# GPS graph layer on one core: the wait for a chunk's gathered rows moved from ScalarE to VectorE

## The chip, the cores and the metric

The kernel runs on one core of one Trainium2 chip (trn2). The metric is the device time of one execution in microseconds (us), the median of three runs. One more execution was recorded by the hardware profiler; all rows in this text are from that one. Engines are named as in the profile: PE (TensorE matrix unit; PEld is its weight load), DVE (VectorE), ACT (ScalarE), POOL (GpSimd), SP (SyncE). A "q" behind the name (DVEq, ACTq, POOLq) is the sequencer of that engine, which handles register, branch and semaphore instructions alone.

## The reference, cut to what matters

The layer adds three things to 6250 node rows of 256 features: a graph attention over 200,000 edges (sorted by destination), a global attention ("mix") and a mixture-of-experts block. The part around the change is the graph attention, together with the mix features that share its loop:

```python
xw = (x @ W).reshape(N, H, C)                 # N = 6250, H = 8, C = 32
e = leaky_relu(a_src[src] + a_dst[dst], 0.2)  # one logit per edge and head
ex = exp(e - m[dst])
alpha = ex / (segment_sum(ex, dst)[dst] + EPS)
out = segment_sum(xw[src] * alpha[:, :, None], dst)   # per destination node
# and per node row of the mix: features of q (products of q with itself), times a fixed matrix
```

The kernel uses, in place of the segment maximum m, a bound per destination (leaky_relu of a_dst plus the largest a_src), and divides once at the end.

## The kernel before, in words

The execution has stages, each a block of its own: weights and statistics, node rows (projection, `node_rows` written to HBM), a short list stage, then the **edge loop** (lines 786 to 1108), then the expert gating, the experts and the last normalisation. The change is in the edge loop.

The sorted edges are cut into 392 chunks of 512 edges (4 tiles of 128). Destinations are cut into 49 blocks of 128 nodes. A chunk that straddles two blocks is worked on once for each, so there are 440 steps (`STEPS`) for 392 chunks. For step s three small tables made by the list stage tell what to take: `blk_row[s]` (the block), `slot_row[s]` (in which of the 4 slots of `rows_g` the chunk lies) and `need_row[s]` (how many chunks must have landed: the chunk's number plus one). An engine reads an entry into a register with `value_load`; the profile shows such a read as TENSOR_LOAD with a few register instructions around it, on the line of the `value_load`.

What each engine does in the loop, in its program order:

- POOL (lines 864 to 890) gathers the source rows. For each chunk it waits until the step that used the slot last has made its messages (`msg_ready`, from DVE), waits for the indices (`idx_in`), issues 4 indirect DMAs (L876, one for each tile of 128 rows of 264 floats), then waits for the landing of the chunk before (`gathered`) and adds one to `chunks_in` (L881).
- SP (L897) loads the index lists, four chunks ahead.
- DVE (`body`, lines 995 to 1015) does for step s: reads `blk_row` (L964) and `slot_row` (L999); `select(s+1)`, four comparisons that make the 0/1 matrix `sel_bf` of the next step (L959); waits for `dst_spread` (the destinations' logits of step s, from PE) and makes the logits `lg` from the gathered rows (L1005, L1007, L1009; `logit_ready`); adds the sums of step s-2 to `acc` (L969); makes one mix feature (`qfeat`, L355); waits for the exponentials (`weight_ready`, from ACT) and makes the messages `msg` (L1015, `msg_ready`).
- ACT (`body`, lines 930 to 944) does for step s: `take_turned(s+1)`, which reads `need_row[s+1]` (L918), waits for `chunks_in` (L919), waits for PE's transposed selection and copies it to `sel_t` (L922); the exponential of the logits of step s (L935); `widen(s+1)`, a copy of `sel_bf` as float32 (L915); the copy of the transposed mix feature (L928). ACT itself reads no gathered row.
- PE (`body`, lines 1075 to 1103) does: `turn(s+1)`, the transposes of `sel_bf` (L1030, `sel_turned`); `aggregate(s-1)`, the sums of messages (L1051, `msg_summed`); transposes of the mix feature (L1058, `feat_turned`); `spread(s+1)`, 12 small products that bring the destinations' logits to the edges (L1042, `dst_spread`); the products of the mix features (L1071).

The last 40 steps have no mix features. The order of the work is set by these programs, written out by hand; nothing is scheduled by a planner. The logits of step s can read the rows safely today because `dst_spread` of step s comes from PE's `spread(s)`, which waits for ACT's `sel_t` copy of step s, which stands behind the chunk wait.

Of the kernel before, what the change touches and what calls it, by code (L numbers as in the profile page):

```python
# [31 lines left out]
CHUNKS = 392  # L32
# [29 lines left out]
def wait(eng, sem, value):  # L62

    if isinstance(value, int) and value <= 0:
        return
    eng.wait_ge(sem, value)
# [48 lines left out]
def gps_layer(nc, x, src, dst, gnn_W, att_src, att_dst, gnn_bias, Wqkv, bqkv, Wproj, bproj, temperature,  # L115
# [3 lines left out]
    def sb(name, shape, dt=F32, ctx=None):  # L119
        return (ctx or top).enter_context(nc.sbuf_tensor(name, shape, dt))  # L120
# [4 lines left out]
    def sem(name, ctx=None):  # L125
        return (ctx or top).enter_context(nc.semaphore(name))

    with top:
# [492 lines left out]
        need_row = sb("need_row", [1, SP_], I32, ctx=early)  # L621
# [165 lines left out]
        with ExitStack() as c:  # L787
# [32 lines left out]
            chunks_in = sem("chunks_in", c)  # L820
# [29 lines left out]
            def units(k):  # L850

                return (H - 1, H) if k == OCT - 1 else (k,)

            def pe_st(j):
                return p_st[:, (j % 2) * TC * P:(j % 2 + 1) * TC * P]

            def p_e(j):
                return p_eb[:, (j % 2) * TC * 2 * H:(j % 2 + 1) * TC * 2 * H]
# [46 lines left out]
            @block.scalar  # L905
            def _(act):
                def query(t):

                    wait(act, q_doubled, t)
                    act.dma_start(qs[:], qn_dram[bass.ts(t, P), :]).then_inc(q_in, 16)  # L910

                def widen(s, j):
                    act.wait_ge(sel_ready, s + 1)
                    wait(act, msg_summed, s - 1)
                    act.copy(sel[j % 2][:], sel_bf[j % 2][:].rearrange("p u d -> p (u d)")).then_inc(sel_wide, 1)  # L915

                def take_turned(s, j):
                    need = act.value_load(need_row[0:1, bass.ds(s, 1)], min_val=1, max_val=CHUNKS)  # L918
                    act.wait_ge(chunks_in, need)  # L919
                    act.wait_ge(sel_turned, s + 1)  # L920
                    wait(act, dst_spread, s - 1)
                    act.copy(sel_t[j % 2][:], pe_st(j)).then_inc(sel_t_ready, 1)  # L922

                def take(n, u):

                    act.wait_ge(feat_turned, n + 1)
                    wait(act, feat_t_used, n - 2)
                    act.copy(feat_t[u % 3][:], p_ft[u % 2][:]).then_inc(feat_t_ready, 1)  # L928

                def body(s, k, tile, last):  # L930
                    j = k % R
                    take_turned(s + 1, j + 1)
                    wait(act, msg_summed, s - 1)
                    act.wait_ge(logit_ready, s + 1)
                    act.activation(msg[j % 2][:, :, D:ROW], lg[j % 2][:], ACT.Exp).then_inc(weight_ready, 1)  # L935
                    widen(s + 1, j + 1)
                    if last is not None and k == 3:
                        act.wait_ge(yt_in_psum, last + 1)
                        act.copy(yt[:], p_o[:, 0:D]).then_inc(yt_ready, 1)
                    if tile is not None:  # L940
                        for u in units(k):
                            take(tile * UNITS + u, u)
                        if k == 1:
                            query(tile + 1)

                query(0)
                widen(0, 0)
                take_turned(0, 0)
                rounds(act, body)
                act.wait_ge(q_in, (T + 1) * 16)  # L950

            @block.vector
            def _(dve):
                def select(s, j):

                    wait(dve, sel_wide, s - 1)
                    wait(dve, sel_turned, s - 1)
                    for u in range(TC):
                        a = dve.tensor_scalar(sel_bf[j % 2][:, u, :], iota_bf[:], dst_t[:, bass.ds(s, 1), u:u + 1].rearrange("p s u -> p (s u)"),  # L959
                                              None, ALU.is_equal)  # L960
                    a.then_inc(sel_ready, 1)

                def block_of(s):
                    return dve.value_load(blk_row[0:1, bass.ds(s, 1)], min_val=0, max_val=T - 1)  # L964

                def accumulate(s, j, b):
                    a = acc[:, bass.ds(b, 1), :].rearrange("p a f -> p (a f)")
                    dve.wait_ge(msg_summed, s + 1)
                    dve.tensor_tensor(a, a, p_m[j % 2][:, 0:ROW], ALU.add).then_inc(acc_added, 1)  # L969

                def query(k, tile, last):
                    if last is not None and k == 1:
                        dve.wait_ge(feat_t_used, last * UNITS + UNITS)
                        y3 = p_y[:, 0:H * V1].rearrange("p (h e) -> p h e", h=H)
                        dve.reciprocal(ry[:], y3[:, :, 0])
                        dve.drain()
                        dve.tensor_tensor(yn[:].rearrange("p (h e) -> p h e", h=H), y3[:, :, 1:V1],
                                          ry[:].unsqueeze(2).broadcast_to([P, H, C]), ALU.mult).then_inc(y_taken, 1)
                    if last is not None and k == 5:
                        r = resid[:, bass.ds(last, 1), :].rearrange("p a f -> p (a f)")  # L980
                        dve.wait_ge(mix_ready, last + 1)
                        dve.tensor_tensor(r, r, p_o[:, 0:D], ALU.add).then_inc(mix_added, 1)
                        dve.drain()
                        dve.tensor_tensor(r, r, b_proj[:], ALU.add)
                    if tile is not None:
                        if k == 0:
                            dve.wait_ge(q_in, tile * 16 + 16)
                            dve.tensor_copy(qq[:, :, 0:C], qs[:].rearrange("p (h e) -> p h e", h=H))
                            dve.tensor_copy(qq[:, :, C:WRAP], qs[:].rearrange("p (h e) -> p h e", h=H)[:, :, 0:WRAP - C]).then_inc(q_doubled, 1)
                            dve.drain()  # L990
                        for u in units(k):
                            wait(dve, feat_turned, tile * UNITS + (u - 2))
                            products(dve, feat[u % 3][:], qq, u).then_inc(feat_ready, 1)

                def body(s, k, tile, last):
                    j = k % R
                    if not (isinstance(s, int) and s < 2):
                        b = block_of(s - 2)
                    slot = dve.value_load(slot_row[0:1, bass.ds(s, 1)], min_val=0, max_val=R - 1)  # L999
                    select(s + 1, j + 1)  # L1000
                    dve.wait_ge(dst_spread, s + 1)
                    g3 = rows_g[:, bass.ds(slot, 1), :, :].rearrange("p a u f -> p (a u) f")
                    pe3 = p_e(j).rearrange("p (u a) -> p u a", u=TC)
                    l = lg[j % 2]
                    dve.tensor_tensor(l[:], g3[:, :, D:ROW], pe3[:, :, 0:H], ALU.add)  # L1005
                    dve.drain()
                    dve.scalar_tensor_tensor(out=l[:], in0=l[:], scalar=SLOPE, in1=l[:], op0=ALU.mult, op1=ALU.max)  # L1007
                    dve.drain()
                    dve.tensor_tensor(l[:], l[:], pe3[:, :, H:2 * H], ALU.subtract).then_inc(logit_ready, 1)  # L1009
                    if not (isinstance(s, int) and s < 2):  # L1010
                        accumulate(s - 2, j - 2, b)
                    query(k, tile, last)
                    dve.wait_ge(weight_ready, s + 1)
                    m4 = msg[j % 2][:, :, 0:D].rearrange("p u (h e) -> p u h e", h=H)
                    dve.tensor_tensor(m4, g3[:, :, 0:D].rearrange("p u (h e) -> p u h e", h=H), msg[j % 2][:, :, D:ROW].unsqueeze(3).broadcast_to([P, TC, H, C]), ALU.mult).then_inc(msg_ready, 1)  # L1015

                select(0, 0)
                rounds(dve, body)
                for s in (STEPS - 2, STEPS - 1):
                    dve.drain()  # L1020
                    accumulate(s, s % R, block_of(s))
                dve.drain()
# [676 lines left out]
```

## Time and profile before

| what | us |
|---|---|
| median of 3 runs | 4702.44 |
| lowest and highest of them | 4685.48 and 4721.66 |
| profiled execution: span from the first to the last instruction | 4647.3 |
| of it, the edge loop's stretch (590 to 3740) | 3150 |

Of the profiled execution only the span is known; what lies around it (start and end of the execution) is the rest of its own time. The span is 55.1 us below the median of the runs. In the profile, the span of an engine's instruction counts as busy; what it waits for is inferred from semaphore events. "remote" is a wait that ended with a semaphore event for which no instruction was found that had just ended; "issue" is idle time with no wait found behind it.

### The profile page before, as it was taken

What the parts mean: (1) busy time and instruction counts of PE and PEld (TensorE: products, weight loads), DVE (VectorE), ACT (ScalarE), POOL (GpSimd) and SP (SyncE); (2) the same over time, 40 slices, a digit from 0 to 9 for tenths busy, and PEclk for the clock granted to TensorE, in tenths of its full rate; (3) what the DMA queues carried; (4) which work ended last, traced back from release to release, by engine and by line L of the source; (5) the groups of instructions that cost most, each with busy time, mean ns of one, the idle gap of its engine ahead of it and who ended that gap; (6) DMA issues with size and microseconds to landing.
All of it is one profiled execution on the core that took longest, in us unless ns stands there. A gap on an engine that the chain in (4) does not pass through costs nothing. (4 is left out here: it accounts for less than half of the span.)

```text
span 4647.3 us, 81992 instructions
## 1 busy us (share of the span) xinstructions
PE 3345.3 (72%) x20995; PEld 2712.4 (58%) x20996; DVE 2450.8 (53%) x6646; ACT 1123.2 (24%) x2618; POOL 2191.8 (47%) x2161
## 2 busy tenths in 40 slices
PE   5888567777777777777778777787776542599950
PEld 2444256666666666666666666666664442488840
DVE  6999745455555555555545545555454484211127
ACT  2333122222222222222222222222222210122210
POOL 3777454544545555444445444454445546200035
PEclk9999767777878787777877777777877755799975
DMA  3000122222222222222222222222222212577743
GB/s 107 28 30 29 24 74 70 69 70 68 71 68 72 71 73 68 69 69 70 71 65 70 70 68 68 68 69 69 70 68 76 70 30 87 190 230 233 235 144 117
DMA packets 276264, 390.98 MB, mean 84 GB/s; under 512 B 113615, under 2 KB 188654, under 8 KB 276184
## 3 DMA queue, kind: packets, MB, share of 16 engines
q0 software_dynamic: 91088, 256.16, 19.7%
q1 hardware_dynamic: 177784, 127.59, 9.4%
q10 hardware_dynamic: 7344, 6.69, 0.5%
q8 instruction: 18, 0.29, 0.0%
q14 instruction: 30, 0.25, 0.0%
HBM read 336.26 MB, written 55.58 MB: 84 GB/s over the span
## 5 line engine op out<-in xcount | busy, mean ns | idle before, releaser
L876 POOL DMA_INDIRECT rows_g<-node_rows,idx x1568 | 1562.5, 996 | 1609.1 <-DVE msg L1015 1131.3
L1051 PE MATMUL p_m<-msg,sel 128*128 128x264 f32 x3520 | 1196.5, 496 | 18.4 <-issue 17.1
L1051 PEld LDWEIGHTS p_m<-msg,sel 128*128 128x128 f32 x3520 | 830.7, 248 | 191.6 <-issue 32.6
L1015 DVE TENSOR_TENSOR msg<-rows_g,msg 128x1024 f32<-128x1024 f32 x440 | 539.4, 1226 | 368.7 <-ACT msg L935 347.3
L1058 PE MATMUL p_ft<-ident,qfeat 128*128 128x128 f32 x1800 | 351.2, 329 | 436.1 <-DVE qfeat L355 386.5
L1005 DVE TENSOR_TENSOR lg<-rows_g,p_e 128x32 f32<-128x32 f32 x440 | 81.1, 184 | 956.1 <-remote 811.8
L1058 PEld LDWEIGHTS p_ft<-ident,qfeat 128*128 128x128 f32 x1800 | 265.9, 175 | 529.3 <-DVE qfeat L355 438.2
L922 ACT COPY sel_t<-p_st 128x512 bf16<-128x512 bf16 x441 | 258.0, 585 | 1254.7 <-remote 814.1
L1071 PE MATMUL p_y<-mix_w,qfeat_t 128*128 128x33 f32 x3200 | 547.4, 324 | 9.3 <-issue 9.3
L1071 PEld LDWEIGHTS p_y<-mix_w,qfeat_t 128*128 128x128 f32 x3200 | 513.4, 244 | 35.5 <-ACT qfeat_t L928 19.8
L915 ACT CAST sel<-sel_bf 128x512 f32<-128x512 bf16 x441 | 270.6, 614 | 688.5 <-PE p_m L1051 408.0
L959 DVE TENSOR_SCALAR sel_bf<-iota_bf,dst_t 128x128 bf16<-128x128 bf16 x1764 | 330.4, 267 | 132.3 <-issue 124.0
L928 ACT COPY qfeat_t<-p_ft 128x512 f32<-128x512 f32 x450 | 263.2, 585 | 408.7 <-PE p_ft L1058 243.7
L1042 PE MATMUL p_e<-adm_parts,sel_t 128*128 x5292 | 225.8, 173 | 173.2 <-ACT sel_t L922 114.1
L1042 PEld LDWEIGHTS p_e<-adm_parts,sel_t 128*128 128x128 bf16 x5292 | 219.3, 101 | 217.2 <-issue 199.5
L1030 PE MATMUL p_st<-ident_bf,sel_bf 128*128 128x128 bf16 x1764 | 210.9, 253 | 103.7 <-DVE sel_bf L959 82.3
L355 DVE TENSOR_TENSOR qfeat<-qq 128x512 f32<-128x512 f32 x400 | 275.0, 688 | 8.9 <-issue 8.6
L1581 POOL DMA_DIRECT2D slot_y<-ysb x64 | 34.6, 541 | 462.9 <-DVE ysb L1571 462.9
L355 DVE TENSOR_TENSOR kfeat<-kk 128x512 f32<-128x512 f32 x250 | 252.9, 1043 | 0.1
L1524 PE MATMUL e_ph<-xst,wa 128*128 128x256 f32 x1024 | 234.5, 382 | 3.5 <-DMA bb<-in_L_ffn_b_dram 2.6
L1533 PE MATMUL e_py<-wb,ht 128*128 128x256 f32 x1024 | 231.4, 379 | 0.0
L1030 PEld LDWEIGHTS p_st<-ident_bf,sel_bf 128*128 128x128 bf16 x1764 | 156.1, 128 | 117.2 <-DVE sel_bf L959 93.1
(294 smaller groups left out, 3816.5 us busy)
## 6 DMA issues: line engine op xcount, KB each, us to landing
wa<-in_L_ffn_w_dram SPq DMA_DIRECT2D x64, 512.0 KB, 3.9
wb<-in_L_ffn_w_dram SPq DMA_DIRECT2D x64, 512.0 KB, 5.2
rows_g<-node_rows,idx POOLq DMA_INDIRECT x1568
xs<-slot_x SPq DMA_DIRECT2D x64, 256.0 KB, 3.2
slot_y<-ysb POOLq DMA_DIRECT2D x64, 256.0 KB, 4.4
bb<-in_L_ffn_b_dram SPq DMA_DIRECT2D x64, 128.0 KB, 5.2
node_rows<-row SPq DMA_DIRECT2D x50, 132.0 KB, 1.8
qs<-qn_dram ACTq DMA_DIRECT2D x51, 128.0 KB
```

Of the source, the lines that this page charges most:

```text
L355: return eng.tensor_tensor(feat.rearrange("p (d i) -> p d i", i=C), bass.AP(base.tensor, base.offset, [whole, [0, DIAGS - 1], [1, C]]), ba ...
L876: pool.indirect_dma_start(rows_g[:, j, u, :], None, node_rows, bass.IndirectOffsetOnAxis(ap=idx[j][:, u:u + 1], axis=0)).then_inc(gathered ...
L915: act.copy(sel[j % 2][:], sel_bf[j % 2][:].rearrange("p u d -> p (u d)")).then_inc(sel_wide, 1)
L922: act.copy(sel_t[j % 2][:], pe_st(j)).then_inc(sel_t_ready, 1)
L928: act.copy(feat_t[u % 3][:], p_ft[u % 2][:]).then_inc(feat_t_ready, 1)
L959: a = dve.tensor_scalar(sel_bf[j % 2][:, u, :], iota_bf[:], dst_t[:, bass.ds(s, 1), u:u + 1].rearrange("p s u -> p (s u)"), None, ALU.is_e ...
L1015: dve.tensor_tensor(m4, g3[:, :, 0:D].rearrange("p u (h e) -> p u h e", h=H), msg[j % 2][:, :, D:ROW].unsqueeze(3).broadcast_to([P, TC, H, ...
L1030: mm = pe.transpose(pe_st(j)[:, u * P:(u + 1) * P], sel_bf[j % 2][:, u, :], ident_bf[:])
L1042: mm = pe.matmul(p_e(j)[:, u * 2 * H:(u + 1) * 2 * H], sel_t[j % 2][:, u * P:(u + 1) * P], adm_parts[:, bass.ds(b, 1), part, :].rearrange( ...
L1051: mm = pe.matmul(p_m[j % 2][:, 0:ROW], sel[j % 2][:, u * P:(u + 1) * P], msg[j % 2][:, u, :], start=(u == 0), stop=(u == TC - 1))
L1058: mm = pe.transpose(p_ft[u % 2][:, m * P:(m + 1) * P], feat[u % 3][:, m * P:(m + 1) * P], ident[:])
L1071: mm = pe.matmul(o, feat_t[u % 3][:, m * P:(m + 1) * P], w, start=False, stop=(u == H and m == FCH - 1), skip_group_check=True)
```

## The change

ACT no longer reads `need_row` and no longer waits for `chunks_in` ahead of the `sel_t` copy. DVE reads `need_row[s]` behind `slot_row[s]` (so ahead of `select(s+1)`) and waits for `chunks_in` behind its wait for `dst_spread`, ahead of the first logit instruction of step s.

```diff
                 def take_turned(s, j):
-                    need = act.value_load(need_row[0:1, bass.ds(s, 1)], min_val=1, max_val=CHUNKS)
-                    act.wait_ge(chunks_in, need)
                     act.wait_ge(sel_turned, s + 1)
                     wait(act, dst_spread, s - 1)
                     act.copy(sel_t[j % 2][:], pe_st(j)).then_inc(sel_t_ready, 1)
...
                     slot = dve.value_load(slot_row[0:1, bass.ds(s, 1)], min_val=0, max_val=R - 1)
+                    need = dve.value_load(need_row[0:1, bass.ds(s, 1)], min_val=1, max_val=CHUNKS)
                     select(s + 1, j + 1)
                     dve.wait_ge(dst_spread, s + 1)
+                    dve.wait_ge(chunks_in, need)
                     g3 = rows_g[:, bass.ds(slot, 1), :, :].rearrange("p a u f -> p (a u) f")
```

## Rows read from the trace of the kernel before

**Rows 1.** Busy time by engine in the edge loop's stretch (us, instructions), granted clock.
```profile
590.00:3740.00 3150.00, 2393.03 (x16371) 2011.59 (x16372) 1607.95 (x4755) 840.16 (x1822) 1560.09 (x1566) 0.77 0.27 70
```

**Rows 2.** Who waited for whom in 590:3740: total us, times, longest.
```profile
POOL rows_g L876 <- DVE msg L1015: 1131.3, 226, 11.2
ACT sel_t L922 <- remote: 814.1, 176, 10.5
DVE lg L1005 <- remote: 811.8, 158, 11.5
...
ACT sel_t L922 <- PE p_st L1030: 395.4, 223, 3.4
...
DVE msg L1015 <- ACT msg L935: 347.3, 209, 7.4
...
DVE lg L1005 <- PE p_e L1042: 130.7, 72, 4.3
DVE sel_bf L959 <- issue: 123.7, 287, 0.9
PE p_e L1042 <- ACT sel_t L922: 114.1, 52, 8.5
...
PE p_st L1030 <- DVE sel_bf L959: 79.3, 70, 2.7
...
ACT sel_t L922 <- issue: 35.3, 37, 4.8
...
ACT sel_t L922 <- POOLq L881: 9.7, 2, 7.8
```

**Rows 3.** Timeline 1968:2002: PE's small products, a gather, and two late releases.
```profile
1981.50 0.45 PE L1042 MATMUL p_e<-adm_parts,sel_t 128*128 x12
...
1984.02 0.94 POOL L876 DMA_INDIRECT rows_g<-node_rows,idx  x1 [0.30 <-issue]
1985.99 0.58 ACT L922 COPY sel_t<-p_st 128x512 bf16<-128x512 bf16 x1 [3.63 <-remote]
1986.06 0.19 DVE L1005 TENSOR_TENSOR lg<-rows_g,p_e 128x32 f32<-128x32 f32 x1 [5.51 <-remote]
```

**Rows 4.** Timeline 2000:2017: a pair of steps.
```profile
2003.72 0.46 PE L1042 MATMUL p_e<-adm_parts,sel_t 128*128 x12
...
2005.14 0.94 POOL L876 DMA_INDIRECT rows_g<-node_rows,idx  x1 [4.06 <-DVE msg L1015]
2005.33 0.18 DVE L1005 TENSOR_TENSOR lg<-rows_g,p_e 128x32 f32<-128x32 f32 x1
...
2007.24 1.22 DVE L1015 TENSOR_TENSOR msg<-rows_g,msg 128x1024 f32<-128x1024 f32 x1 [0.22 <-ACT msg L935]
...
2008.86 0.74 DVE L959 TENSOR_SCALAR sel_bf<-iota_bf,dst_t 128x128 bf16<-128x128 bf16 x4 [0.39 <-issue]
...
2014.60 0.95 POOL L876 DMA_INDIRECT rows_g<-node_rows,idx  x1 [0.30 <-issue]
```

**Rows 5.** Lines L999 (read of slot_row) and L918 (read of need_row): ns min/median/max.
```profile
L999 DVEq FUSED_REGOPS  x493: 53/190/210, 585.1 to 3734.5; - x165
L999 DVEq TENSOR_LOAD <-slot_row x440: 297/300/562, 584.5 to 3734.2; - x147
L999 DVEq SEQ_ASSERT  x440: 23/23/35, 585.3 to 3734.7; - x147
L999 DVEq ALU_OP  x371: 40/40/40, 663.6 to 3734.1; - x186
...
L918 ACTq TENSOR_LOAD <-need_row x441: 273/281/481, 585.1 to 3734.5; - x147
```

**Rows 6.** Timeline 593:604: the first step of the loop.
```profile
593.56 0.58 ACT L922 COPY sel_t<-p_st 128x512 bf16<-128x512 bf16 x1 [7.82 <-POOLq L881]
...
597.66 0.19 DVE L1005 TENSOR_TENSOR lg<-rows_g,p_e 128x32 f32<-128x32 f32 x1 [11.52 <-remote]
```

## The prediction, made before the changed kernel ran

> **What bounds the kernel now.** I read four views: busy time by stretch, then who waited for whom, then timelines of single steps, then the two lines that read a table entry into a register. The edge loop takes 3150 us of the span of 4647.3, and no engine fills it: PE 76%, DVE 51%, POOL 50%, ACT 27%, at a mean granted clock of 0.77, so PE goes part of the time at 2.4 GHz and part at 1.2 [rows 1]. With 440 steps that is 7.16 us for one. The loop is bound by hand-overs between engines, and the question is which of them ends last.
>
> Three waits stand out: POOL's gathers wait 1131.3 us for the messages of DVE, ACT's `sel_t` copy waits 814.1 us for "remote", and so does DVE's first logit instruction, 811.8 us [rows 2]. The copy's line is where the chunk wait stands today, so its 814.1 us invite the reading that ACT sits there until gathered rows land. The rows speak against it. DVE's logit instruction has no chunk wait at present, only the one for `dst_spread` of PE, yet it has the same "remote" share. In one case PE's products ended at 1981.95 by the record, the gather that was under way ended at 1984.96, and DVE and ACT both went on at 1985.99 and 1986.06 [rows 3]. The two wait there for different semaphores of PE. With no gather under way it looks otherwise: PE's products ended at 2004.18, the next gather began at 2005.14 and the logit instruction at 2005.33, with no idle time before it [rows 4]. So I read "remote" as semaphores of PE that reach the others only when a run of gathers is over. Where the chunk wait does end last, the releaser has a name, L881, and that is the case 2 times in 441, 9.7 us in all [rows 2], 7.82 of them at the very first step [rows 6].
>
> The steps go in pairs: a release, a message, then two chunks gathered back to back (here from 2005.14 to 2015.55), while PE's semaphores come late [rows 4].
>
> **The change part by part.**
>
> *The wait itself.* On ACT it costs almost nothing today, so moving it gives almost nothing. On DVE it asks for chunk s just ahead of logits s; ACT asked for chunk s+1 before exponential s, so the new wait is weaker by one step and I count no new wait for rows. Queued behind it on DVE would be the logits, `acc`, the mix feature and the message, and behind the message POOL's next gather; but what passed on ACT in 439 of 441 cases passes on DVE. At the first step something is gained: `sel_t` and PE's products no longer wait for chunk 0, and the logits can start when that is in, near 593.5, and not at 597.66 [rows 6]. That is 4.1 us; as gathers run on there, I keep 0 to 10 and take -5.
>
> *ACT's read goes.* It has one TENSOR_LOAD of 281 ns with register instructions around it [rows 5]. It mostly runs while ACT is busy or waits for PE: the copy waited for PE's transposes 223 times and for "remote" 176 times. Only 37 times, 35.3 us in all, is it late with no releaser [rows 2]. So the gain lies between 0 and 35; not all that time is the read, and I take half, -18.
>
> *DVE's read comes.* DVE's sequencer must do a third read between the message of the step before and `select`. The instructions of one read add up to 300 + 190 + 23 + 40 = 553 ns [rows 5]. From the start of a message (2007.24) to `select` (2008.86) are 1.62 us, in which two reads and two waits stand [rows 4], so one read with its gaps is between 0.55 and 0.81 us; I take 0.69, about the middle. The message covers 1.22 of the 1.62 us, and there is idle time ahead of `select` already: 287 times, 123.7 us, 0.43 each [rows 2]. In these 287 cases nothing covers a third read: 287 x 0.69 = 198 us on DVE's own stream. In the other 153 the sequencer had run ahead, and the read is hidden by the feature and message in front.
>
> How much of the 198 us reaches the end? Counted in two ways. First by PE: its transposes waited for `select` 70 times [rows 2], and each would come 0.69 later: 48 us. Second by DVE: before the logits DVE stood idle 158 + 72 times, with 811.8 + 130.7 us, 4.1 on the mean, which swallows 0.69; in the other 210 of 440 the delay passes, 198 x 210/440 = 95 us. Behind that stands the wait for the exponential, 209 of 440 times with 1.66 us on the mean [rows 2], which swallows as much: 95 x 231/440 = 50 us. What passes delays the message and so, in the worst case, POOL; but in the pair shown POOL was still at the first chunk when the message of the second step ended at 2008.46, so part is covered there too. The two counts agree by chance; they don't add, since they are mostly the same steps. I take 48, and keep 0 (all within waits for PE and for gathers) and 198 (nothing swallowed) as ends.
>
> The Trainium skill has a figure for the read (DMA: Bandwidth & Descriptors, section "Latency and other measured facts"): a `tensor_load` has a floor of some 600 ns. The load here takes 300 ns, half of it; with its register work the read comes near the page's figure. By the page's figure alone, an estimate, the stream would take 287 x 0.6 = 172 us in place of 198.
>
> *The second wait instruction.* Two waits now stand ahead of the logits, so one more sequencer instruction follows a late `dst_spread`. No row shows it alone; the nearest are the 23 and 40 ns of SEQ_ASSERT and ALU_OP [rows 5]. In the 230 steps where the logits waited that is 230 x 0.04 = 9 us, of which I take 8; ends 0 and 20.
>
> *Untouched:* the number of DMAs, their order on POOL and SP, the memory they use.
>
> **The sum.** -5 - 18 + 48 + 8 = +33 us on the profiled execution's span of 4647.3, hence 4680. The execution's own time has in addition what lies around the span, which the change doesn't touch. The runs' median is 55.1 above the span; 4702.4 + 33 = 4735. All ends together reach from -10 - 35 = -45 to +198 + 20 = +218, or 4657 to 4920. A measurement of this kernel tells about 1% (47 us) from no change.
>
> **The rivals.**
>
> *A, the reading of the wait as a gather wait.* If ACT's "remote" 814.1 us were rows on their way, the exponential of step s would stand behind the rows of step s+1 for no reason. The change would free it and the step could shrink by a part of the 4.6 us that one such wait has (814.1/176). With one in four of these saved, 204 us: 4500. For it speaks only the line on which the wait is shown; against it, that DVE has the same wait without asking for chunks, and the 2 times of L881.
>
> *B, the read on DVE decides in full.* The place is DVE's stream from message to `select`; the price is 0.69 us in each of the 287 steps, plus 8: +206 less 23, near +180, or 4885. It decides as soon as the waits that swallow it aren't independent of it: if the 0.69 us moves message and gather alike, the release of PE's semaphores comes 0.69 later too, and the idle time before the logits stays as long as before. For it: POOL waits for the message 226 times of 392. Against it: many messages wait for the exponential, whose time is set by PE and ACT. A half-way form (100 us, 4800) is as likely as the full one.
>
> *C, all hidden, and ACT's gain stands.* DVE's read is lost within waits for PE and the gathers, ACT's read had been on the path (PE's products waited for `sel_t` 52 times, 114.1 us [rows 2]), and the start gains 5: -5 - 18 - some 10 = -33 or 4670.
>
> *D, the change does not do what it says.* The ordering it moves is kept by both forms; then the time moves by the two reads alone, which is my forecast. It has no time of its own.
>
> **How the numbers follow.** Forecast (+0 to +70): 0.48. B, in half or in full (over +70): 0.25. C (0 to -50): 0.22. A: 0.05. The likeliest case's own range is 4702 to 4772. To hold 8 in 10 the range must take in most of C and the half-way form of B: 4665 to 4835. Slower by over 1% (above 4749) is B and two fifths of the forecast: 0.25 + 0.19 = 0.44. Faster by over 1% (below 4655) is A and a third of C: 0.12. Within 1%: 0.44. The point is 4735.
>
> **What would show it.** In the changed kernel's profile the `select` line should have some 0.69 us more idle time before it ("issue", 123.7 us now, some 300 then), in more than 287 steps, and its `need_row` read should stand on DVE's sequencer 440 times. The waits of DVE's logits for L881 should be near none. ACT's "remote" and DVE's should still be there, each near 800 us: had they gone, my reading of them would be wrong and A right. POOL's wait for messages should grow by no more than some 50 us; if it grows by about 200, B is right. The prediction is wrong if the loop's stretch of 3150 us grows by more than 70, or shrinks by more than 50.

## The result, and the profile after

| | before | after |
|---|---|---|
| median of the runs, us | 4712.05 (4 runs, 4685.48 to 4750.91) | 4793.6 (4 runs, 4792.62 to 4805.48) |
| span of the profiled execution, us | 4647.3 | 4792.2 |

The ratio is 1.0147, with a 95% interval of 1.0104 to 1.019: the change made the kernel slower by 69 us of 4712 (the medians are 81.6 apart). The two profiled executions differ by more, 144.9 us, because the one of the kernel before was quicker than all four of its listed runs. (A run of the changed kernel takes only 1.6 us more than its own span, 4793.84 against 4792.2. So the 55.1 us between the span and the median of before are nearly all a difference between two executions, and not time around the span.) So the rows below are to be read for where time went, and the ratio for how much.

The edge loop ended near 3890 in place of 3740. The time before and after it is as it was, within 6 us (902 us after the loop, 907 before). The changed kernel's loop: stretch and its length, busy time of PE, PEld, DVE, ACT and POOL with their instructions, granted clock, share of the DMA engines, GB/s:

```profile
590.00:3890.00 3300.00, 2452.45 (x16349) 2050.53 (x16350) 1604.83 (x4754) 843.22 (x1819) 1554.30 (x1566) 0.76 0.25 67
```

It answers to [rows 1]: nearly the same instructions on each engine and 150 us more. PE's busy time is 59 us longer (150 ns for each instruction against 146, by these two rows), at a granted clock of 0.76 against 0.77, and that of its weight loads 39 us; the other engines' is the same within 6 us. What is new besides are waits. Who waited for whom in the changed kernel's loop (total us, times, longest), in answer to [rows 2]:

```profile
POOL rows_g L876 <- DVE msg L1015: 1300.8, 240, 13.2
DVE lg L1005 <- remote: 779.5, 158, 8.1
ACT sel_t L920 <- remote: 697.8, 153, 12.5
DVE sel_bf L957 <- issue: 506.4, 402, 4.4
ACT sel_t L920 <- PE p_st L1030: 496.9, 229, 4.3
...
DVE msg L1015 <- ACT msg L933: 181.6, 145, 5.6
...
PE p_st L1030 <- DVE sel_bf L957: 156.0, 121, 3.3
...
DVE lg L1005 <- PE p_e L1042: 70.6, 55, 3.2
...
ACT sel_t L920 <- issue: 33.8, 14, 5.5
...
DVE lg L1005 <- POOLq L881: 7.0, 1, 7.0
```

Four things are to be seen. The chunk wait, now on DVE, ended last once, at the first step. The two "remote" waits are still there; the one on ACT, 116 us shorter, outlived the chunk wait that used to stand on its line. Idle time ahead of `select` (L957, the line L959 of before) rose from 123.7 to 506.4 us and from 287 to 402 cases. And PE waited for `select` 121 times, 156.0 us, where it was 70 times and 79.3; POOL's wait for messages rose by 169.5 us.

The idle time ahead of `select` rose by 382.7 us, which is more than 440 reads of 0.69 us. Its longest case is 4.4 us, where it was 0.9. Here is one, on DVE's timeline of the changed kernel:

```profile
1021.33 1.22 DVE L1015 TENSOR_TENSOR msg<-rows_g,msg 128x1024 f32<-128x1024 f32 x1
1026.46 0.74 DVE L957 TENSOR_SCALAR sel_bf<-iota_bf,dst_t 128x128 bf16<-128x128 bf16 x4 [3.91 <-issue]
```

and the same place, the turn from one pass of the loop to the next, in the kernel before:

```profile
1003.94 1.22 DVE L1015 TENSOR_TENSOR msg<-rows_g,msg 128x1024 f32<-128x1024 f32 x1
1005.08 0.73 DVE L959 TENSOR_SCALAR sel_bf<-iota_bf,dst_t 128x128 bf16<-128x128 bf16 x4
```

The branch back is followed by 3.0 us with no instruction on DVE's sequencer (the median of 49 passes, 143.6 us in all, 10.5 before; only the last branch, which leaves the loop, has none). The DMA queues say what it is. The last two lines of that part of the page, after:

```profile
q14 instruction: 270, 2.21, 0.2%
q8 instruction: 18, 0.29, 0.0%
```

Before, the first of them had 30 packets and 0.25 MB. 240 more packets of 8 KB are 4.9 for each of the 49 passes, and one to three of them start within 3.5 us behind each branch, where the kernel before has none: DVE's code is loaded again in each pass. (The expectations below count all packets of this queue, those outside the span and the small ones too: 283 against 43.) The change adds to a pass 8 reads of 4 instructions and 8 waits, 40 instructions. The reads are these rows of the changed kernel (the line of the new read; ns min/median/max):

```profile
L998 DVEq TENSOR_LOAD <-need_row x440: 297/300/324, 585.1 to 3885.5; - x147
L998 DVEq FUSED_REGOPS  x440: 183/183/190, 585.5 to 3885.8; - x147
L998 DVEq SEQ_ASSERT  x440: 23/23/23, 585.7 to 3886.0; - x147
L998 DVEq ALU_OP  x424: 40/40/40, 660.2 to 3885.4; - x142
```

The Trainium skill (Runtime: NRT & Kernel Launch, section "Instruction fetch mechanics") says that the instruction memory of most engines holds two blocks of code, and that a taken branch whose target lies outside them forces a fetch before anything goes on. The trace agrees with the fetch and the stall; its packets are 8 KB, half of the page's block.

So there were two candidates for the loss: the third read ahead of `select`, which the prediction had, and the code loading, which it had not.

### The profile page after: what moved, and what is told of

It reads as the page before. It is cut to its first block and busy times, and to the rows that moved or that the text cites. A ratio compares the mean times of both kernels' runs of the same rounds, so it can differ in the third digit from the quotient of the medians.

```text
span 4792.2 us, 82426 instructions
## 1 busy us (share of the span) xinstructions
PE 3410.6 (71%) x20995; PEld 2756.8 (58%) x20996; DVE 2448.3 (51%) x6646; ACT 1129.9 (24%) x2617; POOL 2174.0 (45%) x2161
## 5 line engine op out<-in xcount | busy, mean ns | idle before, releaser
L1051 PE MATMUL p_m<-msg,sel 128*128 128x264 f32 x3520 | 1228.9, 504 | 69.4 <-issue 68.7
L1051 PEld LDWEIGHTS p_m<-msg,sel 128*128 128x128 f32 x3520 | 845.7, 253 | 250.3 <-issue 86.9
L957 DVE TENSOR_SCALAR sel_bf<-iota_bf,dst_t 128x128 bf16<-128x128 bf16 x1764 | 333.6, 268 | 540.9 <-issue 507.3
L1071 PE MATMUL p_y<-mix_w,qfeat_t 128*128 128x33 f32 x3200 | 559.3, 328 | 3.8 <-issue 3.2
L920 ACT COPY sel_t<-p_st 128x512 bf16<-128x512 bf16 x441 | 259.1, 587 | 1230.7 <-remote 697.8
L1071 PEld LDWEIGHTS p_y<-mix_w,qfeat_t 128*128 128x128 f32 x3200 | 525.2, 249 | 29.8 <-ACT qfeat_t L926 19.2
```

Of the source, the lines that this page charges most:

```text
L1051: mm = pe.matmul(p_m[j % 2][:, 0:ROW], sel[j % 2][:, u * P:(u + 1) * P], msg[j % 2][:, u, :], start=(u == 0), stop=(u == TC - 1))
L1071: mm = pe.matmul(o, feat_t[u % 3][:, m * P:(m + 1) * P], w, start=False, stop=(u == H and m == FCH - 1), skip_group_check=True)
```

## The experiments

Twelve experiments ran, in three sets; two of them, in the second set, repeat kernels that had run already. Each set has its own chip and its own runs of the kernel before, and the ratio is always to these. Medians of before were 4725.06 us in the first set (19 runs), 4645.57 in the second (23 runs) and 3651.76 in the third (13 runs). The third set is so different that it has a part of its own below; times are compared across sets by their ratios alone.

### First set: code loading or the read?

**48 memsets.** On DVE in the list stage, ahead of a wait for DMAs; with the changed kernel.

```diff
+        filler = sb("filler", [1, 256])
...
+                for i in range(48):
+                    dve.memset(filler[:, i:i + 1], 0.0)
                 dve.wait_ge(gcol_in, (4 * FCH + 5) * 16)
```

> The changed kernel, with 48 one-element memsets put on DVE in the list stage, ahead of a wait for DMAs, so that the edge loop's code begins 48 instructions later in DVE's program. Theory 1 (code loading: in the changed kernel DVE's loop back to its first instruction is followed by 3.0 us without an instruction in 49 passes, 143.6 us, against 10.5 us before, and the instruction queue moves 283 packets against 43; the longer loop body lies over one block of code too many): the shift brings the body into fewer blocks, the gap behind the branch falls to some 0.2 us, instruction packets fall to near 45, and the time falls from 4794 to 4700-4750. Theory 2 (the reads alone: 0.69 us of third read ahead of each select, code loading hidden): nothing changes, 4780-4810, and the packets don't matter.

Measured: 4774.42 us, ratio 1.0129 (1.0069 to 1.019). The instruction queue fell back:

```profile
q14 instruction: 30, 0.25, 0.0%
```

and with it the longest idle time ahead of `select` (waits in its loop):

```profile
DVE sel_bf L960 <- issue: 345.6, 391, 1.6
...
PE p_st L1033 <- DVE sel_bf L960: 115.6, 103, 3.3
```

A shift by 48 instructions took all of the reloading away, 161 us of idle time ahead of `select` went (506.4 to 345.6), and most of the slowdown stayed. Theory 1 was right on the mechanism and wrong on its price. With the reloading gone 345.6 us are left ahead of `select`, 222 us more than before.

**The kernel before, with the read alone.** ACT reads and waits as it did; DVE's value is unused.

```diff
                     slot = dve.value_load(slot_row[0:1, bass.ds(s, 1)], min_val=0, max_val=R - 1)
+                    need = dve.value_load(need_row[0:1, bass.ds(s, 1)], min_val=1, max_val=CHUNKS)
                     select(s + 1, j + 1)
```

> The kernel before, ACT as it was (read and wait), and DVE reads need_row as in the changed kernel but doesn't use it. Body of DVE's loop 32 instructions longer than before, 8 shorter than in the changed kernel. If the place of the wait is nothing and the read with its code is all: 4780-4810, as the changed kernel, if the loop's code lies badly here too; 4730-4750 if it lies well (packets tell which). If the wait on DVE costs by itself: clearly less than the changed kernel although packets and the gap behind the branch are as there.

Measured: 4773.68 us, ratio 1.0125 (1.0063 to 1.0188), with 31 packets on the instruction queue, so the code lies well here. The wait stands on ACT and ACT's read is still there, yet the time is that of the run above within 1 us. Its waits:

```profile
DVE sel_bf L959 <- issue: 347.7, 391, 1.6
...
PE p_st L1031 <- DVE sel_bf L959: 118.4, 100, 3.2
```

The read on DVE, ahead of `select`, is the loss: added alone it costs 1.25% (0.6 to 1.9). The place of the wait and ACT's read together make no difference that these runs can tell.

**The read behind `select`.** The changed kernel with 48 memsets, and:

```diff
-                    need = dve.value_load(need_row[0:1, bass.ds(s, 1)], min_val=1, max_val=CHUNKS)
                     select(s + 1, j + 1)
+                    need = dve.value_load(need_row[0:1, bass.ds(s, 1)], min_val=1, max_val=CHUNKS)
```

> As the run with 48 memsets, and DVE reads need_row behind select(s+1) instead of ahead of it. Theory 1 (code loading was most of the loss, the read the rest): idle time ahead of select falls back to near the 123.7 us of before, and the time is 20-60 us below that of the run with the read ahead. Theory 2 (what counts is DVE's whole stream, so the read costs the same wherever it stands): no difference to that run beyond 15 us.

Measured: 4728.05 us, ratio 1.0022 (0.9987 to 1.0056), 46 us less than with the read one line higher. Its waits:

```profile
DVE lg L1008 <- remote: 959.3, 163, 9.3
...
DVE lg L1008 <- issue: 109.9, 197, 6.8
...
DVE sel_bf L960 <- issue: 90.1, 206, 0.9
...
PE p_st L1033 <- DVE sel_bf L960: 51.8, 40, 2.2
...
DVE lg L1008 <- POOLq L884: 24.3, 13, 7.6
```

The same instruction one line lower costs nothing that can be told (at most 0.6% by the interval). The rows agree with this reading: it runs while the engine is at the four comparisons, and where it does come late it is the logits that wait (197 times, 109.9 us), which often wait anyway. DVE also waits for chunks now 13 times, 24.3 us.

**Control: the kernel before with the 48 memsets.**

> Control: the kernel before with the same 48 memsets. The memsets themselves cost at most 3 us; the shorter body fits wherever it lies: gap behind the branch 0.2 us, packets near 43, time within 0.5% of before under both theories. If it moves by more, a shift of the code changes the time in a way other than the one named.

Measured: 4711.31 us, ratio 0.9985 (0.9947 to 1.0024). The shift does nothing that can be told where the code fits. Its idle time ahead of `select` is 129.1 us, so within this set the read put 216 us on top (345.6 in the first kernel of the set).

### Second set: the price of code loading, and which reads may stand where

**The changed kernel again, as it is and with the 48 memsets.**

> The changed kernel as it is, beside the next one on one chip, to weigh the code loading alone. Its DVE stream lost 143.6 us behind 49 branches in the first profile, 133 more than before. If all of that lay on the path it would be 133 us above the next kernel; from the first two calls (4793.6 against 4774.4) I expect 10-35 us, most of the stall hidden in waits for PE and gathers. Packets 283.

> The changed kernel with the 48 memsets again. Packets 43, gap behind the branch 0.2 us. 10-35 us below the run beside it; if the two are the same within 8 us, code loading costs nothing that can be measured and the 1.3% is the read alone.

Measured: the changed kernel 4732.44 us, ratio 1.0175 (1.014 to 1.021), 270 packets; with 48 memsets 4725.64 us, ratio 1.0164 (1.0123 to 1.0204), 30 packets. Idle time ahead of `select` in the first and in the second:

```profile
DVE sel_bf L957 <- issue: 501.9, 396, 4.4
...
PE p_st L1030 <- DVE sel_bf L957: 152.2, 126, 2.9
```

```profile
DVE sel_bf L960 <- issue: 355.8, 394, 1.6
...
PE p_st L1033 <- DVE sel_bf L960: 114.8, 103, 2.8
```

146 us less idle time on DVE, 6.8 us less time, and the intervals lie over each other. My expectation of 10 to 35 us for the code loading was too high: at this place it can't be told from nothing. The earlier difference of 19 us stood between two sets and is not a measurement of it.

**`slot_row`'s read behind `select` too**, in the changed kernel with 48 memsets:

```diff
-                    slot = dve.value_load(slot_row[0:1, bass.ds(s, 1)], min_val=0, max_val=R - 1)
-                    need = dve.value_load(need_row[0:1, bass.ds(s, 1)], min_val=1, max_val=CHUNKS)
                     select(s + 1, j + 1)
+                    slot = dve.value_load(slot_row[0:1, bass.ds(s, 1)], min_val=0, max_val=R - 1)
+                    need = dve.value_load(need_row[0:1, bass.ds(s, 1)], min_val=1, max_val=CHUNKS)
```

> The changed kernel with 48 memsets and both slot_row's and need_row's reads behind select(s+1); only blk_row's stays ahead. If what counts is the time from a message to the next select, this is no worse than the form with one read behind (4728) and its idle time ahead of select goes to near 0; if the logits are as sensitive as select, the two reads behind it (1.38 us against 0.74 us of select) cost again: 4730-4760.

Measured: 4672.14 us, ratio 1.0061 (1.003 to 1.0093). Here no idle time on "issue" is left ahead of `select`, but two reads stand ahead of the logits, which were late on "issue" 198 times for 154.6 us. The kernel is about 27 us slower than before and 54 us quicker than the form with both reads ahead. The form with only `need_row`'s read behind did not run in this set; its ratio in the first, 1.0022 (0.9987 to 1.0056), can't be told from this one.

**The kernel before with `slot_row`'s read behind `select`.**

> The kernel before (ACT waits for the chunk), with slot_row's read behind select(s+1). One read is left under the message (1.22 us against 0.69), one under select. If the 0.43 us ahead of select counts as the third read did (49 us for 0.69 x 391 steps), its 124 us are worth 15-30 us: 4695-4710 where before gives 4725. If the read only moves the stall to the logits: 4715-4735.

Measured: 4651.4 us, ratio 1.0012 (0.998 to 1.0044), nothing gained. Its waits:

```profile
DVE lg L1005 <- issue: 69.9, 110, 5.8
...
PE p_st L1030 <- DVE sel_bf L959: 48.3, 51, 2.9
```

The 123.7 us of idle time ahead of `select` that the kernel before has can be moved to the logits and nothing is gained on balance; what they cost where they stand, this run doesn't part from the 69.9 us that it puts ahead of the logits. The 222 us that the third read puts on top cost 61 to 76 by the ratios (1.0129 of 4725, 1.0164 of 4646). No kernel of the first two sets is clearly faster than before.

### Third set: the same kernel without the late semaphores

> The kernel before, and ACT reads need_row twice ahead of the sel_t copy (the first isn't used): prices the read that the change takes from ACT. My term was 18 us of gain, with 0 and 35 as ends: the doubled read costs 0-35 us, 0 to 0.7%. If ACT's read is as dear as DVE's ahead of select (70-80 us), the change has given back much of its loss there, and this kernel is over 1% slower.

```diff
+                    twice = act.value_load(need_row[0:1, bass.ds(s, 1)], min_val=1, max_val=CHUNKS)
                     need = act.value_load(need_row[0:1, bass.ds(s, 1)], min_val=1, max_val=CHUNKS)
```

Measured: 3660.82 us, ratio 1.0016 (1.0003 to 1.003). A second read on ACT costs some 6 us of 3652 (1 to 11 by the interval).

The kernel before took 3651.76 us in this set, 1000 less than in the others. The profile of this run, which is the kernel before but for that one read, shows what is gone. First 2110 us of its loop, then its waits:

```profile
590.00:2700.00 2110.00, 1898.62 (x15874) 1635.13 (x15874) 1542.30 (x4574) 799.86 (x1762) 1630.67 (x1500) 0.93 0.38 100
```

```profile
ACT sel_t L923 <- POOLq L881: 735.8, 252, 7.8
POOL rows_g L876 <- issue: 492.1, 1545, 2.1
...
ACT sel_t L923 <- PE p_st L1031: 196.1, 178, 3.2
...
PE p_st L1031 <- DVE sel_bf L960: 166.2, 177, 2.9
DVE sel_bf L960 <- issue: 149.6, 345, 0.9
```

There is no "remote" wait on any line, and POOL waited for messages 7 times, 3.9 us in all. POOL gathers nearly all the time (1630.67 us of gathers and 0.3 us between two of them, in 2110), and the chunk wait on ACT, which ended last 2 times in the first profile, does so 252 times. Two steps of this run, with gathers under way all the time:

```profile
2000.73 0.45 PE L1043 MATMUL p_e<-adm_parts,sel_t 128*128 x12
...
2002.16 0.95 POOL L876 DMA_INDIRECT rows_g<-node_rows,idx  x1 [0.30 <-issue]
2002.21 0.18 DVE L1006 TENSOR_TENSOR lg<-rows_g,p_e 128x32 f32<-128x32 f32 x1
```

PE's products ended at 2001.18 and the logits began at 2002.21 behind DVE's comparisons, without idle time, though POOL never paused. In [rows 3] the like took 4.1 us and ended 1.0 us behind a gather.

The traces hold more than these two places. `dst_spread` is counted up once for each group of PE's 12 small products, and the time of each count is in the trace. In the kernel before, of 212 groups that ended while a run of gathers was under way 194 were counted over 0.5 us late (3.4 us on the mean of the 212), of the 225 others 7 (median 0.01 us). In the changed kernel it was 189 of 204 and 2 of 234. In the run of this part it was none of 417 and none of 10. So PE's semaphores come late while gathers run in the profiles of before and of the changed kernel, and not on this chip. But the prediction's "only when a run of gathers is over" is too strong: about half of the late counts of the kernel before (105 of 201) came while the run was still going on. Why gathers go with late semaphores on some chips, and what differs between the chips, no run tells; the granted clock does too (0.93 against 0.77 in the loop).

**The kernel before with an added read behind `select`.**

> The kernel before (ACT reads and waits), and DVE reads need_row behind select(s+1), unused. Against the changed form with the read behind select it differs by ACT's read and the place of the wait only. If what counts is select's own start: within 0.6% of before. If DVE's whole stream counts: 1.3-1.7% above, as with the read ahead of select.

Measured: 3634.06 us, ratio 0.9949 (0.9932 to 0.9966). An added, unused read makes the kernel slightly faster here. With the read behind `select` there is again no cost, and here the interval excludes one. Why it gains stays open; its four runs had a higher granted clock (0.899 to 0.903) than all 13 of before (0.887 to 0.894), and no run tells which comes from which.

**The kernel before with two added reads ahead of `select`.**

> The kernel before, and two unused reads of need_row on DVE ahead of select(s+1): the dose doubled. One read cost 1.25 to 1.6% in three kernels. If waits for PE swallow part and the rest is passed on in full, the second read costs more than the first, since less idle time is left to swallow it: 3.2-4.5% in all. If each costs the same: 2.5-3.2%. Idle time ahead of select near 600 us.

Measured: 4042.02 us, ratio 1.1062 (1.1043 to 1.108), far above both expectations. Its first waits:

```profile
ACT sel L915 <- PE p_m L1053: 774.5, 439, 3.0
DVE sel_bf L959 <- issue: 755.2, 445, 5.4
ACT sel_t L922 <- PE p_st L1032: 754.7, 391, 5.1
POOL rows_g L876 <- DVE msg L1017: 462.2, 129, 9.9
...
PE p_st L1032 <- DVE sel_bf L959: 423.6, 319, 4.3
```

PE waited for `select` 319 times, 423.6 us, against 177 and 166.2 in the run with the doubled read on ACT, and the time grew by 390. The idle time ahead of `select` grew by 606 us against that same run, code loading among it (271 packets, 140 us behind the branches); the 390 us are 64% of that. PE itself was slower too: 130 ns for each instruction of the loop against 120, at a granted clock of 0.85 against 0.93, by estimate 165 us of its busy time. Read in the order of the program, the lateness goes from `select` to PE's transposes, ACT's copy, the exponential and the message. At least three causes of the jump stand side by side, the doubled dose, the code loading and the other chip with its clock; a single read ahead of `select` was not run in this set, so they can't be parted.

**The kernel before with half the gathers.** It leaves out half of the gathered rows.

> The kernel before with two gathers for each chunk in place of four; the rows of the other two tiles are a constant set once, so half of the gathered rows are left out of the result. Theory: semaphores of PE reach the others only when a run of gathers on POOL is over; with 2.5 us of gathers for each chunk in place of 5.0 the waits called remote ahead of the logits and of ACT's copy shrink by half or more (from some 812 and 814 us), and the loop by 400 us or more. Rival (those waits are PE's own work, or a profile artefact): the waits stay within 15% of what they were and the loop gets shorter by less than 150 us.

```diff
-                return (ch - j) * (16 * TC // R) + 16 * TC
+                return (ch - j) * (16 * 2 // R) + 16 * 2
...
-                    for u in range(TC):
+                    for u in range(2):
                         pool.indirect_dma_start(rows_g[:, j, u, :], None, node_rows,
...
+                dve.memset(rows_g[:, :, 2:TC, :], 0.5)
```

Measured: 3318.81 us, ratio 0.9085 (0.9067 to 0.9103). It was made to shrink the "remote" waits, and on this chip there were none, so neither side of its expectation can be judged and it says nothing for or against the late semaphores. What it shows is the next bound: with half the gathers PE is busy 97% of this stretch of the loop at a clock of 0.98.

```profile
590.00:2400.00 1810.00, 1752.84 (x16040) 1557.14 (x16041) 1546.27 (x4637) 826.88 (x1782) 774.87 (x764) 0.98 0.24 61
```

## Why the prediction was right, and where not

The sign, the cause and the range held: 4793.6 against a forecast of 4735 within 4665 to 4835. By the ratio the loss is 69 us (49 to 90) where 33 was forecast, so the likeliest case was too small, and "within 1%" had as much of the chance as what came. Its own mark for being wrong, a loop longer by more than 70 us, was passed in the profiled pair (150), of which part is the quick execution of before.

- *The wait is worth nothing on ACT and nothing on DVE*: right for this chip. L881 ended last once, for 7.0 us at the first step, and the first logits began at 593.53, the 4.1 us earlier that were counted. ACT's "remote" stayed at 697.8 us (814.1 before) without the chunk wait, so rival A is out here. On another chip the same kernel can be as A read it: in the third set the wait on ACT does end last, 735.8 us. The changed kernel did not run there, so what the move would give on that chip stays open.
- *DVE's read*: the right term, mis-sized. The step that was off is the count of 287 cases in which "nothing covers a third read", with the share that reaches the end. I took the cases from the profile of before; with a third read 391 cases have idle time. 345.6 - 123.7 = 222 us were added where 198 were counted, and 61 us (first set, by the ratio) to 76 (second set) reached the end, 27 to 33% of the 222 and 232 added, where 48/198 = 24% was counted. The first count took PE's 70 waits for `select` as fixed, and they became 103 (without code loading); 103 x 0.69 = 71 us, an estimate after the fact, lies within what was measured. The second took the case count from before in the same way. That the two agreed was chance, as the prediction said.
- *ACT's read*: mis-sized. I took a gain of 18; the doubled read costs 6 us on the third chip, where other waits bound the loop, and on the first the kernel with the read on both engines runs as the one with it on DVE alone.
- *The second wait instruction*: 8 us were taken; it goes down in the same comparison, 4773.68 against 4774.42.
- *Not seen at all*: the code loading, 133 us more on DVE's stream. It came out at no cost that could be told (6.8 us), so the sum was not spoiled by it, by luck and not by working.
- *Not in the sum either*: PE's own speed. In the first set the eight runs with the read ahead of `select` had granted clocks of 0.775 to 0.778, the 19 of before 0.778 to 0.786 and the ten with the read behind it 0.776 to 0.786. Whether the lower clock is a part of the loss or comes from PE standing idle longer, no run tells.
- *Rival B*: its full form is out (180), its half-way form (100) is nearer than the forecast (33) in the second set (81 for the changed kernel) and about as near in the result's own pair (69). POOL's wait for messages grew by 169.5 us, nearer to the 200 that stood for B than to the 50 that stood for the forecast; but this pair has the quick execution of before in it. Within the first set that wait was 1245.1 and 1246.9 us with the read ahead of `select` and 1175.1 in the control, some 70 more, which is nearer to the 50.
- *The held semaphores*, on which the reading of the profile rested: the counts of `dst_spread` show that they are late while gathers run (194 of 212 against 7 of 225), though not only until a run of gathers ends. That gathers cause it is not shown: the experiment made for it ran where the lateness doesn't occur.

## What to carry to other kernels

In this loop what a register read cost depended on where it stood: try it first behind an instruction that keeps the engine busy and that others wait for, and not ahead of it. The same read made the kernel 1.3 to 1.6% slower ahead of `select`, and one line lower by nothing that could be told (0.2%). Moving a second read down as well gained nothing. Before a wait is moved, look at who released it: a wait that ends last 2 times in 441 has next to nothing to give on that chip. And when a loop's code grows, compare the instruction queue's packets: a jump by whole packets for each pass points to a reload; here 48 idle instructions ahead of the loop took it away, and the time hardly changed.

## What the runs showed of the hardware that was not expected

- DVE's code was loaded again in each of 49 passes once the loop body was 40 instructions longer: 270 packets of 8 KB against 30, and 3.0 us behind each branch back. A shift of the loop by 48 instructions undid it. With 32 instructions more (281 from one branch to the next, against 289 in the changed kernel) it didn't appear (31 packets).
- One and the same kernel had medians of 4712, 4725, 4646 and 3652 us in four sets of runs. In the profile of before, `dst_spread` was counted up late for 194 of 212 groups that ended during gathers; in the last set, in the run with the doubled read on ACT, for none of 417. A profile from one chip can therefore name another bound than the next chip has: hand-overs during gathers on one, the gathers themselves on the other.
- One read more ahead of `select` in each step, 0.69 us, cost 1.3 to 1.6%; two of them came with 10.6%, though on another chip and with code loading, so how the cost grows with the number of reads isn't shown.
